# A graph transformer block on one core: the work of a slot put in a new order, with adj times x1 behind the transposes, output and expert product together, and probabilities times V last

## What is computed

```
q, k, v = x @ Wq.T, x @ Wk.T, x @ Wv.T          # 16 heads of 32
a = q k^T * D**-0.5 + (adj + adj)               # per head, 128 x 128
p = softmax(a)                                  # rows that are all 0 give 0
x1 = layernorm(x + (p v) @ Wo.T)
top1 = argmax(x1.mean(axis=nodes) @ router_w + router_b)
out = adj @ (x1 @ expert_w[top1])
...
y = relu(batchnorm of out over all graphs of one expert)
result = layernorm(x1 + y)
```

## Time and profile before

| | |
|---|---|
| median of 3 runs | 3041.95 us (3036.92 to 3044.52) |
| the profiled execution's own time | 3046.38 us |
| its span, first to last instruction | 3044.6 us |
| PE busy | 2802.0 us, 92% |
| DVE, ACT, POOL busy | 72%, 58%, 25% |
| mean granted TensorE clock | 0.955 |

### The profile page before, as it was taken

The page is one execution under the profiler, slowest core; times in us unless marked ns, Lnnn a source line. Parts: engine busy times, 40 slices in busy tenths (PEclk is TensorE's granted clock), DMA queues, the critical chain, the costliest instruction groups (busy, mean ns, idle before and its releaser), DMA issues. The chain is left out here.

```text
span 3044.6 us, 70536 instructions
## 1 busy us (share of the span) xinstructions
PE 2802.0 (92%) x24130; PEld 2369.6 (78%) x24130; DVE 2191.3 (72%) x3938; ACT 1772.6 (58%) x6146; POOL 750.3 (25%) x431
## 2 busy tenths in 40 slices
PE   6899999999999999999999999999999999766675
PEld 6788888888888888888888888888888888655554
DVE  7777777777777777777777777777777777628776
ACT  3555655555565555556556555655655555517777
POOL 2022222222222222222222222222222222121111
PEclk9999999999999999999999999999999999867666
DMA  6344444444444444444444444444444444477887
GB/s 224 117 162 173 155 145 172 167 146 162 172 150 150 172 160 146 169 172 145 156 172 159 145 172 166 144 162 172 154 149 172 160 144 162 156 268 265 331 329 267
DMA packets 165115, 537.82 MB, mean 177 GB/s; under 512 B 15539, under 2 KB 48307, under 8 KB 122035
## 3 DMA queue, kind: packets, MB, share of 16 engines
q1 hardware_dynamic: 165042, 536.96, 49.4%
HBM read 427.84 MB, written 109.05 MB: 176 GB/s over the span
## 5 line engine op out<-in xcount | busy, mean ns | idle before, releaser
L548 ACT ACTIVATE prob<-prob,neg_max 128x128 f32<-128x128 f32 x2048 | 795.3, 394 | 361.9 <-DVE abs_max L675 361.9
L323 POOL TENSOR_TENSOR norm<-norm,constants 128x1 f32<-128x1 f32 x128 | 70.8, 553 | 1621.0 <-DVE norm L707 1621.0
L525 ACT ACTIVATE qk<-bank 128x512 f32<-128x512 f32 x256 | 153.1, 599 | 466.1 <-PE bank L343 466.1
L616 DVE SCALAR_TENSOR_TENSOR prob<-bank,adj_in 128x512 f32<-128x512 f32 x512 | 318.0, 684 | 137.0 <-PE bank L343 137.0
L548 ACT ACTIVATION_READ_ACCUMULATOR prob<-prob,neg_max 128x1 f32 x2048 | 394.1, 192 | 0.0
L334 POOL TENSOR_TENSOR moments<-moments,conv 128x1024 f32 x128 | 309.0, 2414 | 328.4 <-ACT conv L573 317.5
L633 DVE TENSOR_TENSOR prob<-prob,inv_sum 128x2048 f32<-128x2048 f32 x128 | 338.8, 2647 | 4.4
L343 PE MATMUL bank<-xT_hi,wq_hi 128*128 128x256 f32 x1024 | 303.4, 296 | 39.9 <-DVE wk_lo L587 19.1
L649 DVE TENSOR_REDUCE neg_max<-prob 128x16 f32<-128x2048 f32 x128 | 291.0, 2274 | 0.0
L343 PE MATMUL bank<-xT_hi,wq_lo 128*128 128x256 f32 x1024 | 290.1, 283 | 0.0
L343 PE MATMUL bank<-xT_lo,wq_hi 128*128 128x256 f32 x1024 | 290.1, 283 | 0.0
(11 more groups left out here) (111 smaller groups left out, 6465.2 us busy)
## 6 DMA issues: line engine op xcount, KB each, us to landing
expert_hi<-expert_hi_scratch SPq DMA_DIRECT2D x128, 1024.0 KB, 4.8
expert_lo<-expert_lo_scratch SPq DMA_DIRECT2D x128, 1024.0 KB, 7.5
xT_in<-xT SPq DMA_DIRECT2D x64, 512.0 KB, 8.5
x_in<-x SPq DMA_DIRECT2D x128, 256.0 KB, 7.9
x_scratch<-x SPq DMA_DIRECT2D x128, 256.0 KB, 8.3
conv_scratch<-conv SPq DMA_DIRECT2D x128, 256.0 KB, 8.4
conv_in<-conv_scratch SPq DMA_DIRECT2D x32, 1024.0 KB, 7.1
x_in<-x_scratch SPq DMA_DIRECT2D x32, 1024.0 KB, 9.1
```

Of the source, the lines that this page charges most:

```text
L525: act.activation(qk[:, npar, c, :, :].rearrange("p k n -> p (k n)"), src[:, :], ACT.Copy).then_inc(qk_copied, 1)
L548: last = act.activation(prob[:, u % 2, h, :], prob[:, u % 2, h, :], ACT.Exp, bias=neg_max2[:, u % 2, h:h + 1], scale=2.0, accum_out=row_su ...
L616: dve.scalar_tensor_tensor(out=prob[:, u % 2, h:HEADS:HPC, :], in0=ps_heads[h][:, :].rearrange("p (c m) -> p c m", c=C), scalar=HALF_SCALE ...
```

## The change

The same operations are done in another order, with another distance in slots for two of the stages. On PE adj times x1 of graph t-3 moves from the end of the slot to right behind the transposes; the output product (graph t-2) and the expert product follow each other, the latter now for graph t-4 instead of t-5; then comes the router, now for graph t-3 instead of t-4; and all four parts of `times_v` (graph t-1) are last. ACT takes oT_hi of graph t-2 first in its slot, and the exponentials of a graph are done in two halves, eight behind the maxima and eight at the start of the next slot; yT_hi stands behind the turned copies, and conv and its square are last. DVE begins with oT_lo, takes both maxima one after the other, then yT_lo, x1 and its norm without a break, and the router last. POOL adds to `moments` before it splits x^T. SP stores conv one slot earlier. One slot less is run at the end (`SLOT_END`).

```diff
-        SLOT_LOOP_START, SLOT_LOOP_END, SLOT_END = 8, B - 8, B + 6
+        SLOT_LOOP_START, SLOT_LOOP_END, SLOT_END = 8, B - 8, B + 5
...
# PE
                 turn(1)
                 turn(2)
                 turn(3)
-                b = t - 4
+
+                b = t - 3
                 if live(b):
-                    if isinstance(b, int) and b == 0:
-                        pe.wait_ge(ld_const, 32)
-                    wait(pe, y_split, b + 1)
+                    p4 = pv_mod(u, -3, 4)
+                    wait(pe, x1_ready, b + 1)
+                    wait(pe, ld_adjT[p4 // 2], 16 * (quarter(i, u, -3) + 1))
+                    if live(t - 2):
+                        wait(pe, oT_split, t - 1)
+                    else:
+                        wait(pe, y_split, b)
+                    wait(pe, expert_known, b)
                     for c in range(C):
-                        last = mm(ps_small[0:1, P + 2:P + 2 + E], sums[:, c:c + 1],
-                                  rw[:, c, :], c == 0, c == C - 1)
-                    last.then_inc(router_done, 1)
-                times_v(0)
-                times_v(1)
+                        lhsT = x1[:, p4 % 2, c * P:(c + 1) * P]
+                        dst = ps_c[:, c * Y:(c + 1) * Y] if c < C - 1 else ps_small[:, 0:Y]
+                        last = mm(dst, lhsT, adjT_in[:, p4 // 2, p4 % 2, :], True, True)
+                    last.then_inc(y_done, 1)
...
-                times_v(2)
-                times_v(3)
-
-                b, y2 = t - 5, pv_mod(u, -5, 2)
+
+                b, y2 = t - 4, u % 2
                 if live(b):
...
# ACT
+                b = t - 2
+                if live(b):
+                    wait(act, pv_done, b + 1)
+                    wait(act, proj_done, b)
+                    act.activation(oT_hi[:, :, :].rearrange("p c n -> p (c n)"), ps_c[:, :],
+                                   ACT.Copy).then_inc(oT_rounded, 1)
+                exps(t - 1, pv_mod(u, -1, 2), HEADS // 2, HEADS)
 
                 copy_qk((2 * u) % C, ps_a)
                 copy_qk((2 * u) % C + 1, ps_b)
```

More of the change, by code:

```diff
@@ L315, in slot @@
                 t = i * 4 + u
[L316 to L324, removed]
                 b = t - 5
@@ L488, in slot @@
                 if live(b):
[L489 to L496, removed]
-                    for c in range(C):
[L498 to L501, removed]
+                    if isinstance(b, int) and b == 0:
+                        pe.wait_ge(ld_const, 32)
+                    wait(pe, y_split, b + 1)
+                    for c in range(C):
+                        last = mm(ps_small[0:1, P + 2:P + 2 + E], sums[:, c:c + 1],
+                                  rw[:, c, :], c == 0, c == C - 1)
+                    last.then_inc(router_done, 1)
+                for c in range(C):
+                    times_v(c)
             run_slots(pe, slot, -2)
@@ L533, in copy_turned, with exps @@
                                        ps_heads[c][:, :], ACT.Copy).then_inc(probT_copied, 1)
+                def exps(b, par2, h0, h1):
+                    if live(b):
+                        for h in range(h0, h1):
+                            last = act.activation(prob[:, par2, h, :], prob[:, par2, h, :], ACT.Exp,
+                                                  bias=neg_max2[:, par2, h:h + 1], scale=2.0,
+                                                  accum_out=row_sum[:, par2, h:h + 1])
+                        if h1 == HEADS:
+                            last.then_inc(exp_done, 1)
+                b = t - 2
+                if live(b):
+                    wait(act, pv_done, b + 1)
[3 more added lines that the diff above has]
+                exps(t - 1, pv_mod(u, -1, 2), HEADS // 2, HEADS)
                 copy_qk((2 * u) % C, ps_a)
@@ L542, in slot @@
                     copy_turned(c)
[L544 to L552, removed]
+                b = t - 3
+                if live(b):
+                    y2 = pv_mod(u, -3, 2)
+                    wait(act, y_done, b + 1)
+                    wait(act, conv_done, b - 1)
+                    act.activation(yT_hi[:, y2, 0:C - 1, :], ps_c[:, 0:(C - 1) * Y].rearrange(
+                        "p (c n) -> p c n", c=C - 1)[:, :, 0:P], ACT.Copy)
+                    act.activation(yT_hi[:, y2, C - 1, :], ps_small[:, 0:P], ACT.Copy).then_inc(y_rounded, 1)
                 if live(t):
@@ L556, in slot @@
                     wait(act, max_doubled, t + 1)
-                exps(0, 6)
-                b = t - 1
+                exps(t, u % 2, 0, HEADS // 2)
+                b = t - 4
                 if live(b):
[L560 to L567, removed]
+                    p2 = u % 2
                     wait(act, conv_done, b + 1)
                     if not isinstance(t, int) or b // 2 > 0:
-                        wait(act, st_conv[p2], 16 * half(i, u, -5))
+                        wait(act, st_conv[p2], 16 * half(i, u, -4))
                     wait(act, moments_added, b - 1)
@@ L608, in slot @@
                 pair, par = half(i, u), u // 2
-                b4 = t - 4
+                b = t - 2
+                if live(b):
+                    wait(dve, oT_rounded, b + 1)
+                    wait(dve, proj_done, b)
+                    dve.tensor_tensor(oT_lo[:, :, :].rearrange("p c n -> p (c n)"), ps_c[:, :],
+                                      oT_hi[:, :, :].rearrange("p c n -> p (c n)").bitcast(F32),
+                                      ALU.subtract).then_inc(oT_split, 1)
                 if live(t):
```

111 lines of the change are left out of this document (50 added, 61 removed).

## The result

The changed kernel takes **2864.22 us**, median of 4 runs (2862.72 to 2866.59); beside it the kernel before takes 3040.76 us (3036.92 to 3044.52, 4 runs). The ratio is 0.9417, 95% interval 0.9406 to 0.9428: 5.8% faster. The profiled executions, 3046.38 and 2865.02, are 181 us apart, where 110 were forecast.

The account below looks back on a forecast made before the run. PE was taken as the bound, with only its losses between groups to win: loop 103, start 4 and end 3 make 110 us, so 3046.4 becomes 2936 profiled and 2932 us median; range 2912 to 2965.

Parts of the forecast that it names:

- nothing changes: Rival: another engine or a chain round the slot sets the loop's pace; median 3042 us, chance 0.03.
- the scores 19.6 to 19.8 apart: Sign that would show the forecast right: successive slots' scores on PE 19.6 to 19.8 us apart in the loop.
- Both waits: PE's losses before q and k (0.35 us, ACT's square of conv) and at adj times x1 (0.37, oT_lo) would go.
- the wait for oT_lo: PE's wait between expert product and adj times x1, sized at 0.37 us a slot, to vanish.
- B: The prediction's junction pricing by product width: 512 wide to small costs 0.09 us, small beside small nothing.
- (1): PE's new slot summed from its pieces without waits: 19.69 us instead of 20.54, 0.85 won, 103 us over 121 slots.
- the 1.84, 1.06 and 1.31: Pieces of PE's slot in us, carried over unchanged: transposes 1.84, adj times x1 1.06, router and PV 1.31.
- The junction output product to expert product: Two 512-wide groups on PE that now touch: priced at 0, with up to 0.10 us allowed.
- Normalising (2): Check for returning waits: normalised probabilities ready before PE's transposes, 2.5 us early, only 0.7 in every other slot.
- The start (3): Slots before the loop: waits for oT_lo in slots 3 and 4 go, slot 5 starts at about 123.2, 4 us won.
- The end (4): From slot 126 on: three last expert products at 12.3 us instead of four at 10.3, longer chain costs 1; 3 us won.
- more room: Claim in the check for returning waits that ACT's and POOL's other pieces have more room than those counted.

## Why the prediction was right in kind and wrong in size

- **PE is the bound, and the gain is what it loses between groups: right.** PE went from 194.66 to 200.00 of 200, and no other engine set a pace. The rival "nothing changes" is gone. Of the signs named, the scores 19.6 to 19.8 apart failed: they are 19.15 apart.
- **Both waits go and none comes back: right.** They were sized at 0.37 and 0.35, read from one slot; measured they are 0.60 (both waits moved) and 0.24 (conv moved). The gap from scores to q and k is about 560, 475, 410 and 325 ns in the four slots of a turn, and I had read the largest. The 0.23 missing from the wait for oT_lo are B's 0.09, the 0.075 by which it also stretched the first step of adj times x1 (left inside the piece of 1.06), and 0.06 because the slot read had a gap of 0.69 where the mean is 0.75. The sum is 0.84; the kernel with both moved won 0.775, and still had 0.06 of the second.
- **The step that failed is in (1): "small to small costs nothing from transposes to router, small to large is counted".** I took the 1.84, 1.06 and 1.31 over as fixed pieces of work and priced junctions by the width of the products. But each of the three holds a change of the weights' shape: transposes to the 1-column router 202 ns where the pace is 109; adj times x1 to the 32-row scores 205; and PV's 32-column tiles on both sides of the output product. Of 5 such junctions (scores to q and k, which stays, not counted) the change leaves two. Over the pace they cost 0.093 + 0.199 + 0.093 + 0.198 + 0.096 = 0.68 before and 0.084 + 0.094 = 0.18 now. That 0.50 stands against the 0.19 forecast; with the 0.84 of the waits against some 0.66 it makes 1.34 of the 1.39 won, where 0.85 were forecast. In the terms of the sum: transposes 1.74 for 1.84, adj times x1 0.81 for 1.06, output product 2.88 for 2.92, expert product 2.83 for 2.85, router and PV 1.18 for 1.31, together 0.54. By experiment, with the same matmuls each time: 0.33 won by putting PV together, 0.37 lost by cutting it again (0.34 without the slower fourth slots), 0.31 lost by the router alone.
- **The junction output product to expert product: right**, 234 ns, free. The range had allowed 0.10 for it. Toward faster the only bounds were 0.05 us a slot and 5 us each for start and end, and the error lay there with 0.54 a slot, which is why the range was too narrow.
- **Normalising (2): right that it does not bind**; the distance in every second slot was 2.8 in the slot shown, not 0.7, since POOL waited for DVE and not DVE for POOL.
- **The start (3)**: 3.8 for 4, but how close that is is partly luck, since slot 5 starts at 123.77, 125.87 or 124.60 in the changed kernel and the two with the same start (router moved at the end, eight more waits). The transposes of slots 3 and 4 wait 2.27 and 1.50 (`DVE prob L643`), which I had not named; before, that of slot 3 waited 2.16 and that of slot 4 did not. **The end (4)**: 6.8 for 3. The last expert products are 10.5, 10.9 and 12.7 apart, forecast 12.3 each; with POOL's old order they are 12.3, 11.8 and 11.7, and by that trace 5 of the 6.8 hang on that order, which the prediction had put under "more room".

What stays open: why these changes cost time, and whether rows and columns count alike. The junctions that pay are 128x128 to 1 or 32 columns and back, 32 columns or 128x128 to 32 rows, and 32 rows to 128x128. From 1 to 32 columns nothing is paid, so it is not just any difference of shape.

The Trainium skill ("TensorE: Matmul & The Clock Gate", "Step-by-step: what each phase is for") says that TensorE brings weight loads ahead of matmuls in flight where the row groups don't conflict or the load goes to the background weights. The rows agree for one shape following itself (load 0.03 to 0.23 ahead, each time right behind the start of the last matmul of the group before). At a change of columns alone, expert product to router, the load was not ahead in any slot seen; by the rule's words it might have been, and there the measurement decides.

## What to carry to other kernels

Where PE is busy almost throughout, look at the idle line of the weight loads put down to "issue" and count how often it comes in a pass: here each was a change of the weights' tile shape or a hidden wait (before, 4 and 1 in every slot, and the wait for conv in every second). Short ones are missing from it, so the starts have the last word. Order the groups so that tiles of one shape are neighbours and odd shapes stand together in one place, as router and PV do; a few tiny matmuls of another shape between two large groups cost more by their place (0.31 us here) than by their work. When one engine holds back PE at two points of a pass, move both: oT_hi alone gave 0.1%, since the time came back at conv, conv alone 0.9%, and both 3.2%.

## What the runs showed that was not expected

- A change of weight shape behind a 512-wide group: 318 to 327 ns where 234 is the pace; between small groups 202 to 205 where 109 is. A 512-wide 128x128 group behind 1 or 32 columns has a first step of 338 to 340 where 233 is the pace. Through a 1-column group the way back is cheaper (router to expert product 96 + 340, and the router's own pace is 25) than through a 32-column one (203 + 338).
- Eight satisfied waits a slot on PE cost nothing (19.148 both).
- Small transfers land sooner in the changed kernel with the same loads. From the page's part on DMA issues, the last column is us to landing:

```profile
x_in<-x SPq DMA_DIRECT2D x128, 256.0 KB, 2.6
x_scratch<-x SPq DMA_DIRECT2D x128, 256.0 KB, 2.1
```

Before they took 7.9 and 8.3. Why is not shown; they may no longer be issued right behind the 1 MB expert loads. No wait of PE in the loop names them, so it is not part of the gain.
